# A fused attention and expert block on one core: x turned by VectorE in 32x32 blocks instead of by TensorE, weights centred once, and a new order for the first block

## The reference, cut to what matters

```python
x = x + _layernorm(attn(_layernorm(x)))
x = x + _layernorm(ffn(_layernorm(x)))
# attn: q, k, v = x @ Wq.T, x @ Wk.T, x @ Wv.T, by heads
#   o = causal linear attention in chunks (state += k^T v)
#   denom = max(|sum(q * cumsum(k))|, 1); o = rmsnorm(o / denom) * norm_w; o @ Wo.T
# ffn: sum over 8 experts of routing weight * (silu(x @ Wg) * (x @ Wu)) @ Wd
```

## Time and profile before

| what | value |
|---|---|
| times of three runs | 1476.43, 1476.51, 1479.62 us, median 1476.51 |
| profiled execution | 1476.86 us, of which the span is 1475.1 us |
| busy share of the span | PE 98%, PEld 86%, DVE 68%, ACT 43%, POOL 29% |
| mean granted TensorE clock | 0.997 of full |
| moved by DMA | 24.58 MB in 25344 packets |
| one block of the loop | some 89 us |

### The profile page before, as it was taken

One profiled execution on the slowest core, in us unless ns is written; L12 is line 12 of the kernel. 1 busy time (PEld: TensorE's weight loads), 2 busy tenths in 40 slices (PEclk: granted clock), 3 DMA queues, 4 the chain that ended last, 5 costly groups with the idle time before them and its releaser, 6 DMA issues. The chain is left out here.

```text
span 1475.1 us, 36709 instructions
## 1 busy us (share of the span) xinstructions
PE 1450.9 (98%) x14182; PEld 1263.7 (86%) x14182; DVE 1000.3 (68%) x2397; ACT 629.5 (43%) x1159; POOL 425.6 (29%) x621
## 2 busy tenths in 40 slices
PE   7899999999999999999999999999999999999997
PEld 6688888888888888888888888888888888888886
DVE  6757667586675767667585675767667676675765
ACT  5434534444353443534445353443534345344432
POOL 2402424123241223414134241232413134241230
PEclk9999999999999999999999999999999999999999
DMA  5100000000000000000000000000000000000000
GB/s 173 58 2 16 15 0 14 14 14 14 0 27 1 14 14 14 14 0 14 14 14 14 0 14 14 14 14 0 28 0 14 14 14 14 0 15 16 1 8 22
DMA packets 25344, 24.58 MB, mean 17 GB/s; under 512 B 2016, under 2 KB 25056, under 8 KB 25312
## 3 DMA queue, kind: packets, MB, share of 16 engines
q1 hardware_dynamic: 25312, 24.13, 5.2%
HBM read 15.74 MB, written 8.39 MB: 16 GB/s over the span
## 5 line engine op out<-in xcount | busy, mean ns | idle before, releaser
L1057 DVE TENSOR_TENSOR late<-late,up_ps 128x512 f32<-128x512 f32 x256 | 175.0, 683 | 145.6 <-PE up_ps L455 113.5
L825 ACT ACTIVATE late<-gate_ps 128x512 f32<-128x512 f32 x256 | 152.6, 596 | 278.0 <-PE gate_ps L455 277.2
L455 PE MATMUL down_ps<-w_hi,h_hi 128*128 128x256 f32 x976 | 264.7, 293 | 0.0
L735 ACT ACTIVATE h_hi<-late 128x512 fp32r<-128x512 f32 x256 | 161.2, 630 | 225.1 <-DVE late L1057 225.0
L455 PE MATMUL down_ps<-w_hi,h_lo 128*128 128x256 f32 x976 | 254.2, 282 | 0.0
L1291 POOL TENSOR_TENSOR rms_in<-rms_in,minus_half 128x16 f32<-128x16 f32 x32 | 93.4, 2918 | 489.5 <-DVE rms_in L1005 489.5
L1079 DVE SCALAR_TENSOR_TENSOR late<-down_ps,route,late 128x256 f32<-128x256 f32 x364 | 158.5, 477 | 86.8 <-PE down_ps L455 84.2
L937 DVE TENSOR_TENSOR h_lo<-late,h_hi 128x512 fp32r<-128x512 f32 x256 | 175.6, 686 | 61.0 <-ACT h_hi L735 61.0
L455 PE MATMUL gate_ps<-ft_hi,w_hi 128*128 128x512 f32 x512 | 204.3, 399 | 1.2 <-ACT ft_hi L735 0.8
L455 PE MATMUL gate_ps<-ft_hi,w_lo 128*128 128x512 f32 x512 | 203.0, 397 | 0.0
L455 PE MATMUL up_ps<-ft_hi,w_hi 128*128 128x512 f32 x512 | 199.7, 390 | 0.0
(11 more groups left out here) (175 smaller groups left out, 2381.7 us busy)
## 6 DMA issues: line engine op xcount, KB each, us to landing
xs<-in_x SPq DMA_DIRECT2D x32, 256.0 KB, 2.8
out_rows<-late SPq DMA_DIRECT2D x32, 256.0 KB, 2.2
late<-in_wg SPq DMA_DIRECT2D x7, 256.0 KB, 2.7
late<-in_wu SPq DMA_DIRECT2D x7, 256.0 KB, 4.4
late<-in_wd SPq DMA_DIRECT2D x6, 256.0 KB, 4.1
late<-in_wkv_t SPq DMA_DIRECT2D x1, 512.0 KB, 4.0
x<-in_wd SPq DMA_DIRECT2D x2, 256.0 KB, 5.6
late<-in_wq_t SPq DMA_DIRECT2D x1, 256.0 KB, 4.7
```

The source lines that it names most:

```text
L455: last = nc.tensor.matmul(dst, lhs, rhs, start=n == 0, stop=n == len(terms + low_terms) - 1)
L735: return nc.scalar.activation(dst, src, ACT.Copy)
L825: nc.scalar.activation(h_f[:, m, :], gate_ps[:, :], ACT.Silu).then_inc(silu_ready[0], 1)
L1057: nc.vector.tensor_tensor(h_f[:, m, :], h_f[:, m, :], up_ps[m][:, :], ALU.mult).then_inc(h_ready[0], 1)
```

## The change

In every block but the first, x is no longer normalised and transposed by PE. SP loads it a second time, by 16 transfers of 32 partitions each, so that each 32x32 block of x lies in one quadrant and DVE's own transpose of 32x32 blocks (four instructions over 128x256) gives x with its columns on the partitions. The buffers are ones that are free at that time (a half of `kz` to load into, `rows` to turn into). High and low part are made from SBUF. The projections use weights whose column mean was taken out once at the start: PE forms the mean with a matrix of 1/256 in `rz`, DVE subtracts it (`centre`). Keys and values get the row's factor `rstd1` when ACT copies them out of PSUM (two instructions each where there was one); queries stay raw, and `norm_stats` bounds the denominator by the row's variance instead of 1. For that the variance has to lie by the layout of the attention's result, and SP carries it there by four small transfers (`place_var`).

In the first block x is normalised as before, but the tables give another order: both halves are transposed before the first projection, and the halves then run step by step. `carry` and the routing's place on POOL move as well.

```diff
-FIRST_PE = [("xt", 0), ("kv", 0), ("q", 0), ("xt", 1), ("su", 0), ("kv", 1), ("kt", 0), ("kt", 1), ("s", 0), ("q", 1), ("su", 1),
-            ("o", 0), ("s", 1), ("o", 1), ("ot", 0), ("wo", 0), ("ot", 1), ("wo", 1), ("ft", 0), ("ft", 1)]
+FIRST_PE = [("xt", 0), ("xt", 1), ("kv", 0), ("kv", 1), ("q", 0), ("su", 0), ("kt", 0), ("su", 1), ("q", 1), ("kt", 1),
+            ("s", 0), ("s", 1), ("o", 0), ("o", 1), ("ot", 0), ("ot", 1), ("wo", 0), ("wo", 1), ("ft", 0), ("ft", 1)]
...
-FIRST_WARM = {("kv", 0): 6, ("s", 1): 2, ("o", 1): 5, ("ot", 0): 5, ("wo", 0): 6, ("ot", 1): 3, ("wo", 1): 6, ("ft", 0): 20}
+FIRST_WARM = {("kv", 0): 3, ("kt", 0): 1, ("su", 1): 2, ("s", 1): 1, ("ot", 0): 16, ("ot", 1): 8, ("ft", 0): 27, ("ft", 1): 3}
...
+            def load_x_t(row):
+                for b in range(B):
+                    for k in range(KT):
+                        for n in range(P // 32):
+                            c = k * P + 32 * n
+                            sp.dma_start(x_blocks[32 * n:32 * n + 32, k, b, :].rearrange("i (a j) -> i a j", j=32),
+                                         x[b, bass.ds(row, ROWS), c:c + 32].rearrange("(a i) j -> i a j", i=32))\
+                                .then_inc(xt_loaded[0], 16)
...
+            def place_var(block):
+                reach(sp, var_ready, block, 0)
+                for g in range(HG):
+                    for i in range(2):
+                        sp.dma_start(var_o[C * g:C * g + C, :, i], var_s[C * i:C * i + C, :], allow_slow_non_contiguous=True).then_inc(var_loaded[0], 16)
...
+            reach(sp, att_done, (0, 0), number_of(("s", 1), (0, 0)) + 1)
+            load_x_t(ROWS)
             reach(sp, x1_ready, (0, 0), 2)
             load_x(ROWS)
+            place_var((1, 0))
             with sp.Fori(1, BLOCKS - 1) as i:
+                reach(sp, blocks_turned, (i, 0), 0)
+                load_x_t(i * ROWS + ROWS)
                 reach(sp, x1_ready, (i, 0), 2)
                 load_x(i * ROWS + ROWS)
+                place_var((i, 1))
                 store_out((i, -1), i * ROWS - ROWS)
...
-                    else:
-                        k = step[1]
-                        reach(pe, xn_ready, a, TILES)
-                        for t in range(TILES):
-                            last = nc.tensor.transpose(dst[:, t // 2, t % 2 * P:t % 2 * P + P],
-                                                       rows[:, t, k * P:k * P + P], ident[:, :])
...
-            warm(14)
+            warm(6)
+            for n, (raw, loaded, columns) in enumerate(((wkv_raw, att_w_loaded[1], 2 * HID), (wq_raw, att_w_loaded[0], HID))):
+                pe.wait_ge(loaded, 16)
+                for k in range(KT):
+                    last = nc.tensor.matmul(up_ps[n][:, 0:columns], rz, raw[:, k, :], start=k == 0, stop=k == KT - 1)
+                last.then_inc(mean_done, 1)
...
+            warm(3)
             pe.wait_ge(w_ready, ATT_W + 3)
             up(0, 0, (0, 0))
...
+                elif kind == "kv" and not is_first(a):
+
+                    reach(act, rstd_ready[0], a, 2)
+                    for b in range(B):
+                        t = 2 * step[1] + b
+                        last = nc.scalar.activation(k_sb[:, t, :], src[:, b, 0:HID], ACT.Copy, scale=rstd1[:, t:t + 1])
+                    last.then_inc(k_ready[0], 1)
...
-                if more:
-                    normalise_x((a[0], a[1] + 1))
                 router_tanh(a)
...
+            def turn_blocks(a):
+                reach(dve, xt_loaded, a, 0)
+                reach(dve, rz_copied, (a[0], a[1] - 1), 1)
+                for k in range(KT):
+                    for b in range(B):
+                        last = nc.vector.transpose(x_t[:, k, b, :], x_blocks[:, k, b, :])
+                last.then_inc(blocks_turned[0], 1)
...
                     hidden(0, m, a)
                     low_hidden(0, m, a)
                     add_down(E - 1, m, f)
+                    if more and m == 0:
+                        turn_blocks((a[0], a[1] + 1))
...
+                elif kind == "centre":
+
+                    raw, n, columns = (wkv_raw, 0, 2 * HID) if p == "wkv" else (wq_raw, 1, HID)
+                    dve.wait_ge(mean_done, n + 1)
+                    nc.vector.tensor_tensor(raw, raw, up_ps[n][:, 0:columns].unsqueeze(1).broadcast_to([P, KT, columns]),
+                                            ALU.subtract).then_inc(w_centred, 1)
```

More of the change, by code:

```diff
@@ L495, in att_step @@
             def att_step(step, a):
+                if step[0] == "xt" and is_first(a):
+                    p = step[1]
+                    pe.wait_ge(xn_ready[0], 2 * p + 2)
+                    for k in range(KT):
+                        for t in range(2):
+                            last = nc.tensor.transpose(att_ps[:, 2 * p + k, t * P:t * P + P], rows[:, 2 * p + t, k * P:k * P + P],
+                                                       ident[:, :])
+                    last.then_inc(xt_done, 1)
                 if step not in PSUM_STEPS:
@@ L905, in _ @@
             high(0, 0, (0, 0))
-            normalise_x((1, 0))
             router_tanh((0, 0))
```

104 lines of the change are left out of this document (64 added, 40 removed).

## The result

The changed kernel takes **1467.4 us** (median of six runs, 1465.73 to 1468.38) where the kernel before takes 1476.5 beside it: a ratio of 0.9936, 95% interval 0.9926 to 0.9947. So it is faster by 9 us. The profiled execution took 1467.63 us, with a span of 1465.9.

What follows compares the result with a forecast made beforehand. PE was taken to bound the loop, a chain of waits the first block. From 1476.9 us, 12.2 for the loop and 2.0 for the first block were subtracted: 1462.7, rounded 1462.5 us, range 1459.0 to 1469.5.

Steps and rivals of the forecast that it cites:

- The loop: Removing PE's transposes of x saves 0.87 us a block, in 14 of the 15 groups, 12.2 us in all.
- The group that gives nothing: Before the loop's first block, eight transposes lie under PE's wait for ScalarE's silu; removing them is worth 0.
- Rival E: No change: another wait stands under the transposes in every block, so the loop gives nothing; 1474.7 us, 5%.
- The turns: VectorE's four 32x32-block transposes a block take 0.35 us each, 1.4 in all, covered up to 2.8 before PE waits.
- Rival D: Slower: turning on VectorE is dear, at 1.2 us an instruction PE waits 2.0 a block; 1492 us, 7%.
- rival B: First block: 128-byte packets of x's second load at 96 ns make VectorE start 6.6 us late once; 1469 us, 12%.
- The first block: From the start to the loop's first gate product: that product comes at 65.7 instead of 67.71, 2.0 us sooner.
- The first projection: In the first block, behind means and centring, it starts at about 14.1 in place of 11.23, 2.9 us later.
- From the projection to the first gate product: First block's attention in the new order, walked through five queues: from about 14.1 to 57.5 (56 to 60).
- rival C: PE pauses about 2 us before the first projection, its clock falls, first block 3 to 5 us worse; 1468 us, 10%.
- The experts at full clock from 55 on: First block's experts run at full clock instead of half; gives back 2.2 us on PE, then silu's chain binds.
- A: The forecast itself, loop and first block as summed: 1462.5 us, own range 1459.5 to 1467, 66%.

Runs made afterwards that it cites:

- e6: Kernel after with the four 32x32 turns of x made twice in a row in every block; 1469.4 us.
- e7: Kernel after with the four 32x32 turns of x made three times in a row in every block; 1494.2 us.
- e8: Kernel after with fewer idle products before the means, x's low part before wo's scaling, 9 pairs before the projections, idle products spread among score and output steps; 1463.8 us.
- e3: Kernel after without centring: the products that form the means and the subtractions are gone; 1463.7 us.
- e1: Kernel before with only the first block's new order and idle products, without raw x and without centring; 1475.5 us.
- e9: Kernel after with 11 pairs of idle products before the key and value products and idle products spread over the score and output steps; 1464.3 us.
- e4: Kernel after with 11 pairs of idle products instead of 3 before the first key and value products; 1463.1 us, again 1464.5 us.
- e2: Kernel after with the first block's order of before, the centring steps put in; 1469.8 us.
- e5: Kernel after with idle products spread over the score and output steps in which PE paused; 1466.3 us.

## Why the prediction was right in the loop and wrong in the first block

**The loop, right.** "0.87 us a block" was 0.85, and "12.2 us" for the 14 groups was 12.58 - 0.31 = 12.27 from the second mark to the last. Of that, 14 x 0.85 = 11.9 is the transposes'; the last period's other 0.34 is none of them and was not traced (that period is 88.14 to 89.08 long in kernels with the same loop), so that the agreement to 0.1 is in part luck. The gate product stands 0.25 behind the last pair, as foreseen.

**The group that gives nothing, right.** The router's transpose is followed by the gate product after 1.23 us both before and after; in the kernel after, the eight transposes are gone and 0.95 us of waiting for silu stands in their place, in the last row of the first block's timeline. Rival E asked whether that happens in every block; it happens in this one only.

**The turns, right.** "0.35 each, 1.4 in all" is 1.41 for four (each 0.41 long, 0.35 in the mean of the four). The cover, "2.8 us", measured by e6 and e7, is 2.7 to 2.8, and what PE waits for beyond it is what was named. The 2.5 us that were estimated from the Trainium skill's VectorE: DVE Perf Modes were too high: in a row of four, twice the width in fp32 cost 1.13 times its 311 ns, not twice. Rival D needs 4.8 us of turning a block for its price; 1.41 is far from that.

**ScalarE, right.** The new passes are 466 and 478 ns long against 477 estimated, and `hidden(0, 1)` no longer waits for ScalarE.

**The transfers, right; rival B out.** In the first block x in 32x32 blocks is issued from 45.18 on, is landed by about 55, and VectorE's statistics at 64.17 don't wait for it. DMA in the kernel after from 179 to 186 us, where nearly all packets are of 128 bytes (the mean is 0.44 MB / 3672 = 120):

```profile
DMA packets 3672, 0.44 MB, mean 63 GB/s; under 512 B 3672, under 2 KB 3672, under 8 KB 3672
...
q1 hardware_dynamic: 3672, 0.44, 40.3%
```

That is 0.403 x 16 x 7 / 3672 = 12.3 ns for a packet, a quarter of the 48 ns for 1 KB, not more than it. The rule on transfers under 512 bytes in the Trainium skill's DMA: Bandwidth & Descriptors did not show here as a price above that of the large packets; per byte they do cost twice as much (0.096 against 0.047 ns).

**The first block, wrong.** "2.0 us sooner" was 3.94 later; at the loop's first gate product, 71.65 where 65.7 stood. The step that failed is the walk from the start to that product, whose terms were too small by 5.95 in sum:
- *The first projection "at about 14.1"* came at 15.61: **1.5**. VectorE's subtraction, which was to begin 5.0 us ahead of the projection, at 9.1, began at 10.36 (its row above), 1.26 later. The means began at 7.02, not 6.4, since the idle products ahead of them outlasted the landing of the weights by 1.3 us (e8 starts them at 5.71), and the part for keys and values took 3.3 us until VectorE began, where 1.9 to 2.9 were given. From there on the chain took 5.25 us where 5.0 were walked. The half of x's normalising that stands in VectorE's queue between the two subtractions cost nothing: the low part that it stands in front of starts at 12.74, and ScalarE's high part, which that needs, ends at 12.68. Of the 4.38 us from 11.23 to 15.61, 3.25 are centring (e3), and the other 1.1 the new order (e1 has 12.46).
- *From the projection to the first gate product, "14.1" to "57.5", 43.4 us.* It took 48.06, **4.66** more. With neither pauses nor a lower clock it takes 44.9 (e9, which has 10 more pairs of idle products on that way), and 44.1 in e4, which has 2.2 us of pauses and the fall at 57. So the walk itself was short by 0.7 to 1.5, and the other 3.2 to 4.0 are the pauses and the lower clock, neither of which was in the sum. Those are what failed: the walk put PE's issuing of small products at nothing, and its clock at full. The wait before the projection was 1.99 us; rival C named it at "about 2 us", and that the clock might fall there. It was right in that: without the wait, no fall there (e4, e9). But the fall costs less than C's price for it: from the projection to the state's products behind (L633) it is 11.06 us in the kernel after and 9.51 in e4 and e9, 1.55 more. It did not foresee the pauses for "issue"; the order before has one of 1.0 us, which was seen only as a small stall. The new order puts the two outputs' small products in one row behind the scores, and the pauses grow to 1.9 to 3.3 us.
- *The experts at full clock from 55 on* was right, and gave back what was expected: 63.67 to 71.65 is 7.98 us against 57.5 to 65.7, 8.2 (**-0.2**).

That the order gains is open. The walk gave it 3.5 us from the projection on (46.9 before, 43.4 foreseen); e1 shows 1.66 at the mark and e2 1.55, each by single profiles whose like differ by up to 3.6. So the time, 1467.4, is A's loop with C's first block. It lies just outside A's own range (1459.5 to 1467), and inside the stated one because that took in C. That C's "3 to 5 us worse than before" is met by 3.94 is luck: its mechanism gave 1.55, and the rest came from the centring's length and from the pauses, which no rival had. The whole was off by 4.9 us, and all of it lies in the first 72 us.

**Which version is best.** e3, e4, e8 and e9 are alike, 1463.1 to 1464.5 us, 1 to 4 us under the kernel after, and e3 leaves out part of the computation. The three kernels without pauses (e5, e8, e9) have lowest and highest run 0.8, 1.0 and 1.7 us apart, the others here 1.5 to 6.7. The smallest edit that gets there is e4's: one number. A ratio to the kernel before of 0.9908 (0.9890 to 0.9926), and 0.9919 (0.9904 to 0.9933) the second time.

**What stays open.** That the pauses are a lack of instructions rests on three things: idle products between the small ones end them (e5, e8, e9), they end 2.2 to 2.8 us behind a fetch, and they stand a fixed number of instructions apart. No run changed the supply itself. How long a pause lasts depends on how much PE still had when the fetch began: in the kernel after its products ran out 0.18 us behind the fetch at 33.20, in e4 1.34 us behind the one at 30.10, and the pauses are 2.05 and 1.15 us. What decides when a fetch begins is open. And a wait of 2.0 us in front of the first projection is followed by the lower clock in all five executions that have it (after, twice, e5, e6, e7), waits of 0.9, 1.4 and 1.7 us there (e3, e1, e2) in none; why is not shown.

## What to carry to other kernels

When work leaves the engine that is the bound, price it by what it delays, from start to start, and check each place where it stands for a wait beneath it: 14 of 15 groups gave 0.87 us, one gave nothing. A new step on another engine is covered by the latest time at which what is queued behind it may start, not by the engine's idle share; doubling and tripling it measures that cover. In a start-up stretch, a path that is only waiting still has a price, since behind a wait of 2 us the clock fell here, and the next 3 us of work went at half speed, which cost 1.5: fill the wait with idle products where it is, and don't add more of them where PE has no time to spare. And profile one program more than once before reading a microsecond from its start: four executions of the same first block ended 3.6 us apart.

## What the runs showed of the hardware

- VectorE turns 128x256 fp32 in 32x32 blocks in 0.41 us, four in a row in 1.41, about what passes of statistics over the same tile take (1.40 for four).
- A packet of 128 bytes took 12 ns of a DMA engine where one of about 1 KB took 48.
- TensorE can outrun its own instructions, by all that these traces show. Rows of small products (64x33, 64x64, 64x66) 17 to 18 ns apart had pauses of 1 to 2.6 us in them with no releaser, in every kernel without spread idle products, and in none of the three with them (e5, e8, e9). The pauses end 2.2 to 2.8 us behind a fetch of instructions and stand 126 products and as many weight loads apart; the page of the kernel after lists the queue, whose fetches are 16 KB each (0.36 MB in 22):

```profile
q8 instruction: 22, 0.36, 0.1%
```

The Trainium skill's Runtime: NRT & Kernel Launch, Instruction fetch mechanics, has the 16 KB blocks, of 256 instructions each, and calls their fetching mostly hidden, since instructions are dispatched more slowly than they are filled in. The row agrees on the size, and 126 products with their weight loads are 252 instructions, besides the few that the profile doesn't count; the pauses of up to 2.6 us say that at this pace the fetching was not hidden.
